# A fused decoder layer on one core: one engine order changed, one input split a period ahead, loops written out

## The chip, the cores and the metric

The kernel runs on one core of one Trainium2 chip. The metric is the device time of one execution in microseconds (us). Engines are named as the profile names them: PE is TensorE, PEld its weight loads, DVE is VectorE, ACT is ScalarE, POOL is GpSimd, SP the engine that issues the transfers. Each engine has its own instruction stream, in order, and they meet through semaphores alone.

## What is computed

Three stages on x of 8 batches x 256 tokens x 512 features, each followed by a residual and a layer norm:

```
i, f, g = x Wi^T, x Wf^T, x Wg^T
h       = scan(h' = sigmoid(f) h + silu(i) (1 - sigmoid(f)))
xg      = h silu(g);  y = xg rsqrt(mean(xg^2) + eps) w_norm;  x1 = LN(x + y Wo)
x2      = LN(x1 + wkv(w, u, k = x1, v = ctx))          # a second scan over the tokens
x3      = LN(x2 + quantised MLP(x2))                   # 512 -> 2 x 1408 -> silu(gate) up -> 512
```

The MLP rounds its input, its hidden row and its weights to 127 steps per row; the kernel multiplies the rounded whole numbers in bf16 and scales behind the product. The first stage's projections are made in three products each, high x high, low x high and high x low, from inputs that are split into a rounded high part and the rest.

## The kernel before

Tiles are 128 tokens; a batch has TB = 2 of them, so 16 tiles n in all. The work is pipelined by hand over three batches. Iteration b runs the MLP of batch b, the middle stage of batch b + 1 and the first stage of batch b + 2, and every engine has a function `iteration` that lists its own steps in order. Ahead of the loop there is a long written-out part (weights are loaded, split or quantised, turned and kept; batches 0 to 2 are started), then `iteration(1, 1)`, then a hardware loop (`Fori(2, 6, 2)`) whose body holds iterations b and b + 1, since the buffers alternate. Batches 6 and 7 end in a written-out tail. In the loop, semaphores are awaited against values worked out from the loop's register.

The steps that the change and the prediction touch:

- PE (line 655, `iteration`): `mlp_up` in three chunks of columns for each of the two tiles, gate and up halves (line 579, 16 products of 128x128 by 512 columns in a full chunk); `turn_keys` (L534); six projections `project` (L476); `turn_hidden` (L599); `mlp_down` (L612) of a tile, 11 products in two parts of 6 and 5 (`PARTS`), each behind its own copy of turned hidden values; `turn_values` (L545); `project_out` (L476) for the tiles 0 and 1; `sum_squares` (L510, 16 tiny products with ones); `turn_inputs` (L554, 8 transposes in 16 bit), which waits for `round_2`.
- ACT (line 984): `split_x` (L835, high part of the next input, 128x1024), `silu` (L929), table loads (L978, L982), `exponential`, `read_projection` (L821 and L824), `split_states` (L841), `square` (L862), `round_hidden` (L936), `read_hidden` (L943), `normalise_3` (L907), `round_2` (L913), `read_inputs` (L920, turned inputs to xqT), `normalise_1` (L901).
- POOL (line 1288): `split_x` (L1189, low part: forget - x_high), `hidden` (L1257, gate x up), `rstd_2` (L1244, L1247), `rms_scale` (L1206), `rstd_1` (L1212 to L1221), `residual_3`, `past_values`, `newton`.
- DVE (line 1693): `scale_products` (L1585, L1588), `weigh_inputs`, `recurrence` (L1440, the scan in the tile `forget`, which also receives the transposed input), `gating` (L1446), `split_states` (L1451), `residual_2`, `layer_norm_2`, `normalise_2` (L1555, two halves of 128x512), `mean_square` (L1457), `scale_2`, `residual_1` (L1465), `layer_norm_1`, `read_down` (L1637), `hidden_max_row` (L1604), `hidden_scale` (L1619 to L1626).
- SP (line 406): transfers of the transposed input (`load_xT`, into `forget`), the context (`load_c`), the input (`load_x`) and two stores of 128 tokens. Each waits for its buffer, and those behind it wait too.

The order at the end of PE's iteration and the start of the next is the one the prediction speaks of:

```
                project_out(b + 2, 0)
                sum_squares(b + 2)
                project_out(b + 2, 1)
                mlp_down(n, 0)
                turn_inputs(b + 1)      # then mlp_up(b + 1, ..., 0, [0])
```

Of the kernel before, what the change touches and what calls it, by code (L numbers as in the profile page):

```python
# [26 lines left out]
BATCHES, T, D, I = 8, 256, 512, 1408  # L27
# [16 lines left out]
PARTS = [(0, (IB + 1) // 2), ((IB + 1) // 2, IB // 2)]  # L44
# [11 lines left out]
def decoder_layer(nc, xT, x, cT, wfT, wiT, wgT, w_norm, woT, w, u, w_gate_up, w_down, out,  # L56
                  scratch):
    ctx = ExitStack()
    with ctx:
# [286 lines left out]
        def _(sp):  # L346
            def load_xT(b):
                wait(sp, h_ready, b)
                sp.dma_start(forget[:, :, :], xT[b]).then_inc(xT_loaded, 16)
# [56 lines left out]
            def iteration(b):  # L406
                load_xT(b + 2)
                load_c(b + 1)
                store(b * TB - 2, b - 1, 0)
                load_x(b + 2)  # L410
                store(b * TB - 1, b - 1, 1)
# [38 lines left out]

            with sp.Fori(1, BATCHES - 2) as b:
                iteration(b)
# [15 lines left out]
        def _(pe):  # L468
# [135 lines left out]

            def mlp_down(n, t):

                s = (t + NC) % 2
                pe.wait_ge(mlp_read, chunks_read(n))
                for part, (first, count) in enumerate(PARTS):
# [4 lines left out]
                last.then_inc(down_done, 1)  # L614

# [39 lines left out]
            def iteration(b, par):  # L655
# [20 lines left out]
                turn_hidden(n, 0, 0)  # L676
                turn_hidden(n, 0, 1)
                project_out(b + 2, 0)
                sum_squares(b + 2)
                project_out(b + 2, 1)  # L680
                mlp_down(n, 0)
                turn_inputs(b + 1)

            pe.wait_ge(identity_ready, 1)
# [81 lines left out]

            iteration(1, 1)
            with pe.Fori(2, BATCHES - 2, 2) as b:
                iteration(b, 0)
                iteration(b + 1, 1)  # L770

# [36 lines left out]
        def _(act):  # L808
# [175 lines left out]
            def iteration(b, par):  # L984
                n = b * TB
                split_x(b + 2)
                silu(b, par, 0, [0])
# [31 lines left out]
                read_hidden(n, 0, 1)  # L1019
                silu(b, par, 1, [2])  # L1020
                normalise_3(n - 1, 1)
                round_2(b + 1, 1 - par, 0)
# [91 lines left out]
            silu(0, 0, 0, [2])  # L1114
            square(2)
            round_hidden(0, 0, 0)
            round_hidden(0, 0, 1)
# [9 lines left out]

            iteration(1, 1)
            with act.Fori(2, BATCHES - 2, 2) as b:
                iteration(b, 0)  # L1130
                iteration(b + 1, 1)

# [53 lines left out]
        def _(pool):  # L1186
# [101 lines left out]
            def iteration(b, par):  # L1288
                n = b * TB
                split_x(b + 2)  # L1290
                residual_3(n - 2, 1 - par, 0)
# [14 lines left out]
                rms_scale(b + 2)  # L1306
                hidden(b, 1, [2])
                rstd_1(b + 2)

# [50 lines left out]
            hidden(0, 0, [2])  # L1360
            rstd_2(1)
            rms_scale(2)
            hidden(0, 1, [0])
# [3 lines left out]

            iteration(1, 1)
            with pool.Fori(2, BATCHES - 2, 2) as b:
                iteration(b, 0)  # L1370
                iteration(b + 1, 1)

# [32 lines left out]
        def _(dve):  # L1405
# [422 lines left out]

            iteration(1, 1)
            with dve.Fori(2, BATCHES - 2, 2) as b:  # L1830
                iteration(b, 0)
                iteration(b + 1, 1)

# [111 lines left out]
```

## Time and profile before

| | |
|---|---|
| median of 3 executions | 435.67 us (434.51 to 436.34) |
| the profiled execution | 435.61 us |
| its span, first to last instruction | 433.8 us |
| mean granted TensorE clock | 0.977 of 2.4 GHz |
| PE busy | 386.3 us, 89% |
| DVE busy | 364.1 us, 84% |
| ACT busy | 320.3 us, 74% |
| POOL busy | 217.1 us, 50% |
| transfers | 31.75 MB, 73 GB/s on average |

The 1.8 us between span and time lie around the first and last instruction. Busy shares are means over a start in which weights come in, a repeating middle (from about 148 to 368 us, batches 1 to 5) and a tail with little PE work. In a timeline row the first two numbers are start and length of a merged run of like instructions, `x4` their count, and the bracket the idle time of the engine ahead of it and what ended it. Lengths of merged matmuls carry a pipeline's tail of about 0.17 us.

### The profile page before, as it was taken

The page shows a single profiled execution, that of the slowest core. Times are in us where ns is not written, and L with a number is a line of the kernel's source. Part 1 is how long each engine was busy: PE and PEld are TensorE (multiplying, and loading weights), DVE is VectorE, ACT ScalarE, POOL GpSimd, SP SyncE. Part 2 cuts the span into 40 slices and gives each one's busy share as a digit, 9 for nine tenths or more (in the row PEclk, how much of TensorE's full clock was granted, in tenths as well). Part 3 has the DMA queues.
Part 4 walks back from the last instruction along what each step waited for, and adds up shares of the span by engine and source line. Part 5 has one row for each costly group of instructions (what it writes and reads, how often), then busy time and mean ns, then how long its engine had stood idle before and what let it go on. Part 6 is the DMA issues. An engine that isn't in the chain of part 4 may idle for free.

```text
span 433.8 us, 8164 instructions
## 1 busy us (share of the span) xinstructions
PE 386.3 (89%) x2906; PEld 305.5 (70%) x2906; DVE 364.1 (84%) x620; ACT 320.3 (74%) x422; POOL 217.1 (50%) x266
## 2 busy tenths in 40 slices
PE   7898989989898899989998999899989998577873
PEld 7797889877876597759774977597758776333431
DVE  3879698493998799989898998899888989899684
ACT  3668678639926799589957996699759884986671
POOL 1554465243542865457435942594258436626451
PEclk9899999989999999999999999999999999888998
DMA  7946350663020002030203020302030202000101
GB/s 261 351 165 244 115 214 20 232 50 91 2 98 1 2 0 75 2 122 2 73 2 122 3 74 0 121 0 73 0 121 0 73 0 73 2 25 2 48 13 62
DMA packets 12843, 31.75 MB, mean 73 GB/s; under 512 B 2038, under 2 KB 5132, under 8 KB 12812
## 3 DMA queue, kind: packets, MB, share of 16 engines
q1 hardware_dynamic: 12812, 31.35, 21.8%
q8 instruction: 18, 0.29, 0.3%
q14 instruction: 13, 0.11, 0.1%
HBM read 27.14 MB, written 4.21 MB: 72 GB/s over the span
## 4 chain that ended last, share of the span: by engine, by line
PE 43%; ACT 18%; DVE 15%; issue 12%; POOL 5%; DMA 3%; SPq 1%; ACTq 0%; POOLq 0%; DVEq 0%
PE proj_ps L476 24%; PE slot_ps L579 10%; PE slot_ps L612 3%; PE turn_ps L510 2%; POOL ring L1257 2%; ACT xqT L920 2%; DVE ring L1585 2%; ACT L978 2%; ACT hqT L943 2%; DMA ring<-w_gate_up_dram 2%; DMA ring<-w_down_dram 2%; DVE ring L1588 2%; ACT turn_ps L883 2%; ACT L982 1%; DVE xg_low L1451 1%
## 5 line engine op out<-in xcount | busy, mean ns | idle before, releaser
L579 PE MATMUL slot_ps<-w1q,xqT 128*128 128x512 bf16 (+1 forms) x384 | 83.1, 367 | 10.5 <-ACT xqT L920 7.6
L1257 POOL TENSOR_TENSOR ring<-ring 128x512 f32<-128x512 f32 (+1 forms) x48 | 60.5, 1263 | 33.6 <-ACT ring L929 33.6
L579 PEld LDWEIGHTS slot_ps<-w1q,xqT 128*128 128x128 bf16 x384 | 36.8, 99 | 48.8 <-issue 7.9
L476 PE MATMUL proj_ps<-x_high,proj_high 128*128 128x256 f32 x384 | 65.8, 294 | 2.1 <-DVE inp L1465 2.0
L476 PE MATMUL proj_ps<-x_high,proj_low 128*128 128x256 f32 x384 | 62.5, 285 | 0.0
L476 PE MATMUL proj_ps<-x_low,proj_high 128*128 128x256 f32 x384 | 62.4, 284 | 0.0
L476 PEld LDWEIGHTS proj_ps<-x_high,proj_high 128*128 128x128 f32 x384 | 54.2, 192 | 3.9 <-issue 2.4
L476 PEld LDWEIGHTS proj_ps<-x_high,proj_low 128*128 128x128 f32 x384 | 53.9, 193 | 0.0
L476 PEld LDWEIGHTS proj_ps<-x_low,proj_high 128*128 128x128 f32 x384 | 53.4, 191 | 0.0
L929 ACT ACTIVATE ring<-ring,zero_bias,x_scale 128x512 f32<-128x512 f32 (+1 forms) x48 | 36.9, 774 | 12.3 <-DVE ring L1585 11.8
L612 PE MATMUL slot_ps<-w2q,hqT 128*128 128x512 bf16 x176 | 42.1, 388 | 4.3 <-ACT hqT L943 3.3
L1585 DVE TENSOR_TENSOR ring<-slot_ps,scale_rows 128x512 f32<-128x512 f32 (+1 forms) x48 | 30.7, 639 | 17.0 <-PE slot_ps L579 17.0
L1232 POOL TENSOR_TENSOR den<-den,q_state 128x512 f32<-128x512 f32 x16 | 26.4, 1657 | 34.7 <-ACT q_state L889 34.4
L1199 POOL TENSOR_SCALAR ring<-ring,row_inv 128x512 f32<-128x512 f32 (+1 forms) x26 | 27.2, 1060 | 19.1 <-DVE row_inv L1680 19.1
L936 ACT ACTIVATE ring<-ring,round_bias,hid_inv 128x768 f32<-128x768 f32 (+1 forms) x32 | 29.6, 965 | 7.1 <-DVE hid_inv L1626 7.1
L612 PEld LDWEIGHTS slot_ps<-w2q,hqT 128*128 128x128 bf16 x176 | 16.2, 99 | 25.1 <-issue 5.2
L1588 DVE TENSOR_TENSOR ring<-slot_ps,scale_rows 128x512 f32<-128x512 f32 (+1 forms) x48 | 30.5, 636 | 0.0
L1189 POOL TENSOR_TENSOR x_low<-forget,x_high 128x1024 fp32r<-128x1024 f32 x7 | 16.6, 2370 | 26.7 <-ACT x_high L835 26.7
L1604 DVE TENSOR_REDUCE hid_top<-ring 128x1 f32<-128x1408 f32 x15 | 24.2, 1611 | 5.5 <-POOL ring L1257 5.4
L943 ACT ACTIVATE hqT<-slot_ps,half_bias 128x768 bf16<-128x768 f16 (+1 forms) x32 | 25.3, 836 | 4.1 <-PE slot_ps L599 4.1
L1227 POOL TENSOR_TENSOR num<-num,c_sb 128x512 f32<-128x512 f32 x16 | 20.3, 1284 | 11.7 <-ACT num L873 11.4
L1674 DVE TENSOR_REDUCE row_max<-ring 128x2 f32<-128x1024 f32 (+1 forms) x15 | 19.8, 1317 | 5.9 <-DMA ring<-w_down_dram 4.8
(133 smaller groups left out, 845.7 us busy)
## 6 DMA issues: line engine op xcount, KB each, us to landing
ring<-w_gate_up_dram SPq DMA_DIRECT2D x11, 512.0 KB, 5.0
forget<-xT_dram SPq DMA_DIRECT2D x8, 512.0 KB, 3.9
x_sb<-x_dram SPq DMA_DIRECT2D x8, 512.0 KB, 3.7
c_sb<-cT_dram SPq DMA_DIRECT2D x8, 512.0 KB, 4.1
out_dram<-z SPq DMA_DIRECT2D x16, 256.0 KB, 2.0
ring<-w_down_dram SPq DMA_DIRECT2D x4, 704.0 KB, 5.7
scale_rows<-scratch_dram SPq DMA_DIRECT2D x2, 704.0 KB, 5.9
x<-wfT_dram SPq DMA_DIRECT2D x2, 512.0 KB, 5.6
```

The lines of the kernel that those rows point to most:

```text
L476: last = nc.tensor.matmul(out, a, b, start=(i == 0), stop=(i == len(terms) - 1))
L579: last = nc.tensor.matmul(slot_ps[:, s, half * 512:half * 512 + width], xqT[:, par, d, t * P:(t + 1) * P], w1q[:, d, half * I + at:half * ...
L612: last = nc.tensor.matmul(slot_ps[:, s, 0:D], hqT[:, i, :], w2q[:, i, :], start=(i == 0), stop=(i == IB - 1))
L929: nc.scalar.activation(g, g, ACT.Silu, bias=zero_bias[:, :], scale=x2_scale[:, par, t:t + 1]).then_inc(silu_ready, 1)
L936: nc.scalar.activation(h, h, ACT.Identity, bias=round_bias[:, :], scale=hid_inv[:, t:t + 1]).then_inc(hid_rounded, 1)
L943: nc.scalar.activation(hqT[:, first:first + count, :].rearrange("p i t -> p (i t)"), part_16((t + 1 + NC) % 2, part), ACT.Identity, bias=h ...
L1199: last = nc.gpsimd.tensor_scalar(rows[:, a, :], rows[:, a, :], row_inv[:, c:c + 1], ROUND, ALU.mult, ALU.add)
L1232: nc.gpsimd.tensor_tensor(blocks(den, h), blocks(den, h), blocks(rec_copy, h), ALU.mult).then_inc(newton_ready, 1)
L1257: nc.gpsimd.tensor_tensor(hid, hid, gate_buf[:, at:at + width], ALU.mult).then_inc(hid_ready, 1)
L1585: nc.vector.tensor_tensor(gate_buf[:, at:at + width], slot_ps[:, s, 0:width], scale_rows[:, at:at + width], ALU.mult).then_inc(gate_scaled, 1)
L1588: nc.vector.tensor_tensor(hid_buf(t)[:, at:at + width], slot_ps[:, s, 512:512 + width], scale_rows[:, I + at:I + at + width], ALU.mult).th ...
L1604: nc.vector.tensor_reduce(hid_top[:, :], hid_buf(t)[:, 0:I], AX.X, ALU.max, apply_absolute_value=True).then_inc(hid_top_ready, 1)
```

## The change

PE does `sum_squares(b + 2)` ahead of both `project_out`, and `turn_inputs(b + 1)` between the two parts of `mlp_down(n, 0)`; `mlp_down` takes the parts as an argument for that. `split_x` for batch b + 3 moves from the start of iteration b + 1 to the end of iteration b on ACT (ahead of `normalise_3`) and POOL (ahead of `rstd_1`), and that of batch 3 into the part ahead of the loop (ACT behind `square(2)`, POOL behind `rstd_2(1)`). Its transfer is issued in iteration b, behind the first store, and `load_x` ahead of that store. The hardware loops of all five engines become Python loops, so each iteration's instructions are written out, with constants.

```
@@ -404,10 +404,11 @@
                 sp.dma_start(out[b, par], y3[:, par, :]).then_inc(out_stored[par], 16)
 
             def iteration(b):
-                load_xT(b + 2)
                 load_c(b + 1)
+                load_x(b + 2)
                 store(b * TB - 2, b - 1, 0)
-                load_x(b + 2)
+                if b + 3 < BATCHES:
+                    load_xT(b + 3)
                 store(b * TB - 1, b - 1, 1)
 
 
@@ -448,7 +449,8 @@
             spread_scales(2)
             load_x(2)
 
-            with sp.Fori(1, BATCHES - 2) as b:
+            load_xT(3)
+            for b in range(1, BATCHES - 2):
                 iteration(b)
 
 
@@ -602,16 +604,19 @@
                                                identity16[:, :])
                 last.then_inc(hq_turned, 1)
 
-            def mlp_down(n, t):
+            def mlp_down(n, t, parts=(0, 1)):
 
                 s = (t + NC) % 2
-                pe.wait_ge(mlp_read, chunks_read(n))
-                for part, (first, count) in enumerate(PARTS):
+                if parts[0] == 0:
+                    pe.wait_ge(mlp_read, chunks_read(n))
+                for part in parts:
+                    first, count = PARTS[part]
                     pe.wait_ge(hq_ready, 2 * n + part + 1)
                     for i in range(first, first + count):
                         last = nc.tensor.matmul(slot_ps[:, s, 0:D], hqT[:, i, :], w2q[:, i, :],
                                                 start=(i == 0), stop=(i == IB - 1))
-                last.then_inc(down_done, 1)
+                if parts[-1] == 1:
+                    last.then_inc(down_done, 1)
 
             def turn_rows(q):
 
@@ -675,11 +680,12 @@
                 turn_values(b + 1, 1)
                 turn_hidden(n, 0, 0)
                 turn_hidden(n, 0, 1)
+                sum_squares(b + 2)
                 project_out(b + 2, 0)
-                sum_squares(b + 2)
                 project_out(b + 2, 1)
-                mlp_down(n, 0)
+                mlp_down(n, 0, (0,))
                 turn_inputs(b + 1)
+                mlp_down(n, 0, (1,))
 
             pe.wait_ge(identity_ready, 1)
 
@@ -764,10 +770,8 @@
             turn_inputs(1)
             mlp_down(0, 0)
 
-            iteration(1, 1)
-            with pe.Fori(2, BATCHES - 2, 2) as b:
-                iteration(b, 0)
-                iteration(b + 1, 1)
+            for b in range(1, BATCHES - 2):
+                iteration(b, b % 2)
 
 
             mlp_up(6, 0, 0, [0])
@@ -983,7 +987,6 @@
 
             def iteration(b, par):
                 n = b * TB
-                split_x(b + 2)
                 silu(b, par, 0, [0])
                 exp_tables()
                 exponential(b + 1, 0)
@@ -1018,6 +1021,8 @@
                 read_hidden(n, 0, 0)
                 read_hidden(n, 0, 1)
                 silu(b, par, 1, [2])
+                if b + 3 < BATCHES:
+                    split_x(b + 3)
                 normalise_3(n - 1, 1)
                 round_2(b + 1, 1 - par, 0)
                 round_2(b + 1, 1 - par, 1)
@@ -1113,6 +1118,7 @@
             split_states(2)
             silu(0, 0, 0, [2])
             square(2)
+            split_x(3)
             round_hidden(0, 0, 0)
             round_hidden(0, 0, 1)
             silu(0, 0, 1, [0])
@@ -1125,10 +1131,8 @@
             silu(0, 0, 1, [2])
             normalise_1(2)
 
-            iteration(1, 1)
-            with act.Fori(2, BATCHES - 2, 2) as b:
-                iteration(b, 0)
-                iteration(b + 1, 1)
+            for b in range(1, BATCHES - 2):
+                iteration(b, b % 2)
 
 
             exp_tables()
@@ -1287,7 +1291,6 @@
 
             def iteration(b, par):
                 n = b * TB
-                split_x(b + 2)
                 residual_3(n - 2, 1 - par, 0)
                 hidden(b, 0, [0])
                 past_values(b + 1, 0)
@@ -1305,6 +1308,8 @@
                 rstd_3(n - 1, 1)
                 rms_scale(b + 2)
                 hidden(b, 1, [2])
+                if b + 3 < BATCHES:
+                    split_x(b + 3)
                 rstd_1(b + 2)
 
             nc.gpsimd.memset(ones[:, :], 1.0)
@@ -1359,16 +1364,15 @@
             hidden(0, 0, [1])
             hidden(0, 0, [2])
             rstd_2(1)
+            split_x(3)
             rms_scale(2)
             hidden(0, 1, [0])
             hidden(0, 1, [1])
             rstd_1(2)
             hidden(0, 1, [2])
 
-            iteration(1, 1)
-            with pool.Fori(2, BATCHES - 2, 2) as b:
-                iteration(b, 0)
-                iteration(b + 1, 1)
+            for b in range(1, BATCHES - 2):
+                iteration(b, b % 2)
 
 
             residual_3(10, 1, 0)
@@ -1826,10 +1830,8 @@
             layer_norm_1(2)
             read_down(0, 0, 0)
 
-            iteration(1, 1)
-            with dve.Fori(2, BATCHES - 2, 2) as b:
-                iteration(b, 0)
-                iteration(b + 1, 1)
+            for b in range(1, BATCHES - 2):
+                iteration(b, b % 2)
 
 
             hidden_max_row(5, 1)
```

## Rows read from the trace of the kernel before

**Rows 1.** Windows, PE alone: stretch, length, PE busy (instructions), granted clock, DMA share, GB/s.
```profile
148.00:176.00 28.00, 27.95 (x217) 1.00 0.09 30
283.00:311.00 28.00, 27.82 (x216) 1.00 0.08 28
```

**Rows 2.** Timeline of PE, loop: start us, us, engine line, instruction, xcount [idle before].
```profile
278.29 3.62 PE L579 MATMUL slot_ps<-w1q,xqT 128*128 128x512 bf16 x16 [1.30 <-ACT xqT L920]
...
311.46 1.20 PE L476 MATMUL proj_ps<-wo_high,xg_high 128*128 128x512 f32 x4 [0.64 <-DVE xg_low L1451]
...
318.98 2.55 PE L612 MATMUL slot_ps<-w2q,hqT 128*128 128x512 bf16 x11
...
323.25 1.03 PE L579 MATMUL slot_ps<-w1q,xqT 128*128 128x512 bf16 x4 [1.28 <-ACT xqT L920]
```

**Rows 3.** Timeline of ACT over the same period.
```profile
278.32 1.52 ACT L901 ACTIVATE x<-inp,shift,rstd 128x512 f32<-128x512 f32 x2 [0.18 <-POOL shift L1221]
...
281.05 0.81 ACT L929 ACTIVATE ring<-ring,zero_bias,x_scale 128x512 f32<-128x512 f32 x1 [0.17 <-DVE ring L1585]
...
292.83 0.69 ACT L824 ACTIVATE inp<-proj_ps,zero_bias 128x512 f32<-128x512 f32 x1 [1.04 <-PE proj_ps L476]
...
317.92 0.82 ACT L907 ACTIVATE z<-z,shift,rstd 128x512 f32<-128x512 f32 x1 [2.63 <-POOL shift L1278]
318.86 1.52 ACT L913 ACTIVATE num<-x,round_bias,x_inv 128x512 f32<-128x512 f32 x2
322.01 1.11 ACT L920 ACTIVATE xqT<-turn_ps,half_bias 128x1024 bf16<-128x1024 f16 x1 [1.63 <-PE turn_ps L554]
```

**Rows 4.** Timeline of DVE over the same period.
```profile
307.54 1.25 DVE L1446 TENSOR_TENSOR inp<-inp,gate 128x1024 f32<-128x1024 f32 x1 [0.67 <-ACT gate L824]
...
315.19 1.95 DVE L1555 TENSOR_SCALAR x<-num,mv,rstd 128x512 f32<-128x512 f32 x2 [0.18 <-POOL rstd L1247]
```

**Rows 5.** Timeline of ACT behind the loop: round_2 and read_inputs of batch 7.
```profile
398.03 1.51 ACT L913 ACTIVATE num<-x,round_bias,x_inv 128x512 f32<-128x512 f32 x2
400.25 1.11 ACT L920 ACTIVATE xqT<-turn_ps,half_bias 128x1024 bf16<-128x1024 f16 x1 [0.71 <-PE turn_ps L554]
```

**Rows 6.** Timeline of POOL in the loop.
```profile
280.96 2.37 POOL L1189 TENSOR_TENSOR x_low<-forget,x_high 128x1024 fp32r<-128x1024 f32 x1 [2.67 <-ACT x_high L835]
...
315.12 1.27 POOL L1257 TENSOR_TENSOR ring<-ring 128x512 f32<-128x512 f32 x1
...
321.97 0.20 POOL L1212 TENSOR_TENSOR ve<-mv,eps_col 128x2 f32<-128x2 f32 x1 [2.40 <-DVE mv L1477]
```

**Rows 7.** Timeline of DVE behind the loop: read_down and the last of hidden_scale.
```profile
366.76 0.74 DVE L1637 SCALAR_TENSOR_TENSOR z<-slot_ps,hid_scale,scale_rows 128x512 f32<-128x512 f32 x1
...
369.51 0.21 DVE L1626 TENSOR_SCALAR hid_inv<-hid_rec,x_scale 128x1 f32<-128x1 f32 x1
```

**Rows 8.** DMA issues of the page: KB each, median us from issue to landing.
```profile
forget<-xT_dram SPq DMA_DIRECT2D x8, 512.0 KB, 3.9
```

**Rows 9.** Timelines of ACT, POOL, DVE and PE ahead of the loop.
```profile
131.99 1.84 ACT L936 ACTIVATE ring<-ring,round_bias,hid_inv 128x768 f32<-128x768 f32 x2 [4.29 <-DVE hid_inv L1626]
...
131.76 0.69 POOL L1247 TENSOR_TENSOR rstd<-ve,minus_half 128x2 f32<-128x2 f32 x1
...
138.18 0.69 POOL L1206 TENSOR_TENSOR rms<-msq,minus_half 128x2 f32<-128x2 f32 x1 [5.72 <-DVE msq L1457]
...
132.49 1.00 DVE L1555 TENSOR_SCALAR x<-num,mv,rstd 128x512 f32<-128x512 f32 x2 [0.53 <-POOL rstd L1247]
...
134.75 1.47 PE L579 MATMUL slot_ps<-w1q,xqT 128*128 128x384 bf16 x8 [0.79 <-DVE ring L1588]
```

**Rows 10.** Timeline of PE behind the loop.
```profile
377.93 0.82 PE L599 MATMUL slot_ps<-identity,ring 128*128 128x128 f16 x6 [3.95 <-ACT ring L936]
...
380.92 3.72 PE L612 MATMUL slot_ps<-w2q,hqT 128*128 128x512 bf16 x11 [0.16 <-ACT hqT L943]
```

**Rows 11.** Source query of L1465: durations ns min/median/max, first and last start, forms.
```profile
L1465 DVE SCALAR_TENSOR_TENSOR inp<-proj_ps,rms,x_sb x16: 732/750/752, 44.4 to 364.6; 128x512 f32<-128x512 f32 x16
```

More of the change, by code:

```diff
@@ L406, in iteration @@
             def iteration(b):
-                load_xT(b + 2)
                 load_c(b + 1)
+                load_x(b + 2)
                 store(b * TB - 2, b - 1, 0)
-                load_x(b + 2)
+                if b + 3 < BATCHES:
+                    load_xT(b + 3)
                 store(b * TB - 1, b - 1, 1)
@@ L449, in _ @@
             load_x(2)
-            with sp.Fori(1, BATCHES - 2) as b:
+            load_xT(3)
+            for b in range(1, BATCHES - 2):
                 iteration(b)
@@ L603, in turn_hidden, with mlp_down @@
                 last.then_inc(hq_turned, 1)
-            def mlp_down(n, t):
+            def mlp_down(n, t, parts=(0, 1)):
                 s = (t + NC) % 2
-                pe.wait_ge(mlp_read, chunks_read(n))
-                for part, (first, count) in enumerate(PARTS):
+                if parts[0] == 0:
+                    pe.wait_ge(mlp_read, chunks_read(n))
+                for part in parts:
+                    first, count = PARTS[part]
                     pe.wait_ge(hq_ready, 2 * n + part + 1)
@@ L613, in mlp_down @@
                                                 start=(i == 0), stop=(i == IB - 1))
-                last.then_inc(down_done, 1)
+                if parts[-1] == 1:
+                    last.then_inc(down_done, 1)
             def turn_rows(q):
@@ L677, in iteration @@
                 turn_hidden(n, 0, 1)
+                sum_squares(b + 2)
                 project_out(b + 2, 0)
-                sum_squares(b + 2)
                 project_out(b + 2, 1)
-                mlp_down(n, 0)
+                mlp_down(n, 0, (0,))
                 turn_inputs(b + 1)
+                mlp_down(n, 0, (1,))
             pe.wait_ge(identity_ready, 1)
@@ L765, in _ @@
             mlp_down(0, 0)
[L767 to L770, printed above, removed]
+            for b in range(1, BATCHES - 2):
+                iteration(b, b % 2)
             mlp_up(6, 0, 0, [0])
@@ L985, in iteration @@
                 n = b * TB
-                split_x(b + 2)
                 silu(b, par, 0, [0])
@@ L1020, in iteration @@
                 silu(b, par, 1, [2])
+                if b + 3 < BATCHES:
+                    split_x(b + 3)
                 normalise_3(n - 1, 1)
@@ L1115, in _ @@
             square(2)
+            split_x(3)
             round_hidden(0, 0, 0)
@@ L1126, in _ @@
             normalise_1(2)
[L1128 to L1131, printed above, removed]
+            for b in range(1, BATCHES - 2):
+                iteration(b, b % 2)
             exp_tables()
@@ L1289, in iteration @@
                 n = b * TB
-                split_x(b + 2)
                 residual_3(n - 2, 1 - par, 0)
@@ L1307, in iteration @@
                 hidden(b, 1, [2])
+                if b + 3 < BATCHES:
+                    split_x(b + 3)
                 rstd_1(b + 2)
@@ L1361, in _ @@
             rstd_2(1)
+            split_x(3)
             rms_scale(2)
@@ L1366, in _ @@
             hidden(0, 1, [2])
[L1368 to L1371, printed above, removed]
+            for b in range(1, BATCHES - 2):
+                iteration(b, b % 2)
             residual_3(10, 1, 0)
@@ L1827, in _ @@
             read_down(0, 0, 0)
[L1829 to L1832, printed above, removed]
+            for b in range(1, BATCHES - 2):
+                iteration(b, b % 2)
             hidden_max_row(5, 1)
```

## The prediction

> **What bounds the kernel now.** I read the PE rows of the windows first, then the timelines of the four engines over one batch period of the loop, then the same engines just ahead of the loop and behind it. In the repeating part TensorE is nearly always at work: 27.82 of 28 us in a looped stretch and 27.95 of 28 in the same stretch of batch 1, which is straight-line code [rows 1]. One period, from the first gate/up product to the next one, takes 323.25 - 278.29 = 44.96 us, and there are two holes in it: 0.64 us before `project_out`, waiting for VectorE's xg_low, and 1.28 us before the first `mlp_up`, where PE has turned the inputs and waits for ScalarE to copy them out [rows 2]. So a period is PE's work plus a wait that PE's own order causes: `mlp_down` stands ahead of `turn_inputs`, and nothing stands behind it.
>
> Call R the end of `round_2`, which releases `turn_inputs`: 318.86 + 1.52 = 320.38 [rows 3]. From the period's first product (278.29) to R there are 42.09 us, in this chain: 14.54 to ScalarE's read of the third projection (292.83, where it had been idle for 1.04, so PE is the later one), then ScalarE, VectorE and ScalarE back to back with holes of 0.7 at most [rows 2 to 4]. From R to the next first product the old order takes 44.96 - 42.09 = 2.87 us.
>
> **The change, part by part.**
>
> *`turn_inputs` between the two parts of `mlp_down`.* The six products of part 0 take 6 x 0.217 = 1.30 us (eleven take 2.55 less about 0.17 of tail, [rows 2]). They end at 318.98 + 1.30 = 320.28, before R, so the turn now starts at R. Behind the loop there is a turn that is not queued behind other work: `round_2` ends at 398.03 + 1.51 = 399.54 and ScalarE's copy starts at 400.25, 0.71 later [rows 5]. The copy takes 1.11, and from its end to PE's product there are 323.25 - (322.01 + 1.11) = 0.13 in the loop [rows 2, 3]. R to first product becomes 0.71 + 1.11 + 0.13 = 1.95; the five products of part 1 (1.09) lie under the copy. The period becomes 42.09 + 1.95 = 44.04, a gain of 0.92 us.
>
> Who is late next? `read_down` on VectorE now waits for part 1: 0.71 for the turn with its handovers and 1.09 of products, so R + 1.8. VectorE's statistics are done at R + 1.6 (POOL's rstd starts on them at 321.97, [rows 6]), so it waits 0.2 us. From `read_down` to the free gate product takes 369.72 - 366.76 = 2.96 [rows 7], and the gate product that releases silu is another 0.7: silu at R + 5.5. ScalarE's front of silu, exponentials and two projection reads takes 292.83 - 1.04 - 281.05 = 10.74 [rows 3], ready at R + 16.2. PE delivers the third projection at R + 1.95 + 14.54 = R + 16.5. PE is still the later, by 0.3: the gain holds, but no more than 0.3 above it is to be had.
>
> *`sum_squares` ahead of `project_out`.* It waits for ScalarE's squares instead of xg_low, both made from the same product at about the same time, and can win at most the first hole of 0.64 [rows 2]. But the 7.52 us of products up to 318.98 and part 0 would then only end before 320.28 and wait longer for R; mean_square is queued behind normalise_2 on VectorE and is not late. Should the squares come later than xg_low, there are 0.10 us before part 0 passes R. Worth nothing now; bounds -0.1 and +0.1 a period.
>
> *`split_x` one period ahead.* ScalarE's 1.13 us leave the start of the period and land ahead of `normalise_3`, where it is idle for 2.63 [rows 3]. POOL's 2.37 us leave 280.96 and land before rstd_1, where POOL is idle for 2.40 [rows 6]; that fits within 0.1 us. The normalised rows behind it are there at 278.32 + 1.52 = 279.84, and `turn_keys` wants them 3.62 us behind the first product, at 281.91 [rows 2, 3]: of these 2.07 us some 1.0 are left when PE starts 0.92 earlier. Nothing is gained at the start of the period, since silu waits for VectorE; it only keeps x_low from becoming late for a PE that starts 0.9 earlier. Its DMA needs the recurrence's end, before 307.54, and a store ahead of it whose rows are ready sooner, and takes 3.9 to land [rows 4, 8], against a split at about 315. SP's load of x now follows that of c at once; both buffers are free by then, and c is read only behind silu and the table load. Zero for both.
>
> *Loops written out.* Constant waits can save the 0.08 by which the loop's handover is longer than 0.05, at one place of the chain; more code has to be fetched, but batch 1 already runs as straight code with PE as full as in the loop [rows 1]. I take 0; bounds: -0.3 in all, and above it the 0.13 by which the two stretches differ in each of four periods, +0.5.
>
> *The new `split_x(3)` ahead of the loop.* On ScalarE it falls into 4.29 us of idling. On POOL it stands right behind rstd_2(1), which ends at 132.45, ahead of a 5.72 us wait: free for POOL. But the same rstd_2 releases VectorE's normalise_2, at 132.49 [rows 9]. In the loop the same pair meets: a POOL product of 1.27 us starts at 315.12, 0.07 ahead of normalise_2, and the two VectorE halves take 1.95 us [rows 4, 6]. Ahead of the loop, with POOL quiet, they take 1.00 [rows 9]. The first half would be done at 315.74 and is done 0.95 later, 0.30 after the POOL product's end at 316.39. Behind a POOL instruction of 2.37 us that starts at about 132.43, the first half ends at 132.43 + 2.37 + 0.30 = 135.10 instead of 133.04: +2.06 us. Everything here hangs on it: PE waits for the scaled product behind normalise_2 (0.79 at 134.75, [rows 9]), then come sum_squares, residual, hidden maximum, and silu of batch 1. No slack is in it. Bounds: 0 if VectorE starts first; 2.4 if it waits out the whole instruction and then runs in full.
>
> The Trainium skill ("SBUF — State Buffer", section "SBUF: two separate sides") gives GpSimd and a VectorE operation in a two-port mode one shared port pair, which whoever starts first keeps for its whole instruction. By that rule the price is 2.0 us with POOL first and nothing with VectorE first, the sum 434.0 or 432.0. By that rule, the trace agrees as far as POOL first goes; no row here shows VectorE first against an instruction of this length.
>
> **Sum.** R of batch 1 is set by the ScalarE-VectorE chain, not by PE: it gains nothing and moves by +2.06. From there to R of batch 5 there are four periods: -4 x 0.92 = -3.7. The fifth early start (batch 6) gives nothing: its second product group stands behind `turn_keys`, whose rows come 279.84 - 278.29 = 1.55 us after the old first product, so 2.5 after the new one, with one product group of 1.8 us ahead of it. Bounds for it: 0 to 0.9. Total -1.6. The profiled execution took 435.61 us, 0.06 under the median of 435.67: forecast **434.0 us**.
>
> **Rivals.**
> *No collision ahead of the loop* (VectorE starts first, or waits less): 435.67 - 3.7 = 432.0. For: the two are released by one event, 0.06 apart. Against: POOL was first in the loop, where it too had no other wait.
> *TensorE's clock falls ahead of the loop.* PE's idle before 134.75 grows from 0.79 to 2.83. Behind the loop, after 3.95 us of idling, eleven products took 3.72 instead of 2.55 us [rows 2, 10]: half the clock, 1.2 of 2.4 GHz. If the 3 us around sum_squares run at half clock, 1.3 to 1.7 us come on top: 435.5. Against: this idle is shorter, and batch 1 runs at full clock behind it now [rows 1].
> *Slower: x_low blocks VectorE in the loop too.* Its new place is over residual_1 and the statistics. If residual_1 waited it out as normalise_2 does, about 2 us, `read_down` would come at R + 3.6, silu at R + 7.3, the third read at R + 18.0 instead of 16.5: period 45.5, +0.6 x 4 = 2.4, and 2.06 before it: 440.1. It decides as soon as VectorE loses over 0.5 us (0.2 of idling and 0.3 of PE's lead). Against: residual_1 took 0.732 to 0.752 in all sixteen cases, with and without POOL beside it [rows 11].
> *The loop gains nothing* (VectorE or POOL's Newton step, which has 0.67 us of slack before the gating product [rows 4], takes over): 435.67 + 2.0 = 437.7.
>
> **Numbers.** Forecast 0.50, no collision 0.20, clock 0.15, slower by x_low 0.05, no gain in the loop 0.10. A measurement tells about 0.5% from no change, 2.2 us: 433.5 and 437.85 are the limits. The forecast's own range is 433.0 to 434.9, so a quarter of it counts as faster, with all of the no-collision case: 0.32. Slower are x_low's case and a third of the last, 0.08. Same: 0.60. The range runs from 431.6 (no collision, with the 0.3 of the written-out loops) to 436.9 (clock, or half the loop's gain missing).
>
> **What would show it.** Right: periods of about 44.0 us, the hole before `mlp_up` between 0.1 and 0.3 us with one of some 0.1 to 0.5 before `turn_inputs`; the two halves of normalise_2(1) at about 3.0 us with x_low started just ahead; `round_2` of batch 1 about 2 us later than before, of batch 5 about 1.7 earlier. Wrong: normalise_2(1) at 1.0 us; periods above 44.3; residual_1 above 0.9 us; a granted clock under 1 between 136 and 145.

## The result, and the profile after

The changed kernel takes 450.46 us (median of 4 executions, 447.81 to 452.41); the kernel before took 435.28 beside it (434.51 to 436.34, 4 executions). The ratio is 1.033, 95% interval 1.030 to 1.037. It is slower by 15 us where 434.0 had been forecast, with 0.08 given to slower at all.

| | before | after |
|---|---|---|
| profiled execution, its span | 435.61, 433.8 us | 451.22, 449.2 us |
| mean granted clock of TensorE | 0.977 | 0.948 |
| first product of batch 1 (gate/up) | 141.71 | 145.34 |
| period of batches 1 to 5 | 46.64, 44.96, 44.98, 44.96, 44.89 | 49.17, 44.87, 46.39, 47.99, 48.02 |
| behind the fifth period | 65.7 | 67.4 |

So of 15.4 us of span, 3.6 come ahead of the loop, 10.0 in its five periods (236.44 against 226.43), 1.8 behind. The 3.6 and the 1.8 are less firm than the 10.0: in nine profiled kernels that have no collision ahead of the loop, the kernel before among them, the first product of batch 1 lies anywhere from 139.13 to 141.71, and *loops_only*, with the old order, already takes 66.8 behind the fifth period. I did not follow up the part behind. The periods are not alike, which a wait alone would make them. The timeline of PE over the end of one period, in the changed kernel:

```profile
316.51 1.04 PE L547 MATMUL turn_ps<-identity,num 128*128 128x128 f32 x8
317.59 0.78 PE L601 MATMUL slot_ps<-identity,ring 128*128 128x128 f16 x11
320.04 2.73 PE L512 MATMUL turn_ps<-ones,gate 128*128 128x1 f32 x16 [1.67 <-DVE num L1540]
322.62 2.05 PE L478 MATMUL proj_ps<-wo_high,xg_high 128*128 128x512 f32 x4
324.47 1.91 PE L478 MATMUL proj_ps<-wo_high,xg_low 128*128 128x512 f32 x4
326.18 1.82 PE L478 MATMUL proj_ps<-wo_low,xg_high 128*128 128x512 f32 x4
327.83 1.09 PE L478 MATMUL proj_ps<-wo_high,xg_high 128*128 128x512 f32 x4
```

Two things are to be seen. First, `sum_squares` (L512) waits 1.67 us, and not for the squares but for `num` of L1540, VectorE's `residual_2`. Second, behind that hole the same work takes longer: four products of `project_out` 1.8 to 2.05 us instead of 1.1 to 1.2. That is the lower clock, as the windows say (stretch, length, PE busy, granted clock, DMA share, GB/s), first over the slow products, then over a whole period without a fall, one with a short one and one with a long one:

```profile
319.50:327.50 8.00, 7.46 (x28) 0.59 0.06 21
194.51:239.38 44.87, 42.82 (x298) 1.00 0.13 45
239.38:285.77 46.39, 44.35 (x297) 0.96 0.14 47
285.77:333.76 47.99, 45.95 (x297) 0.93 0.14 46
```

VectorE over the same stretch shows why the releaser is late, and who waits next:

```profile
317.47 1.23 DVE L1455 TENSOR_TENSOR xg_low<-inp,xg_high 128x1024 fp32r<-128x1024 f32 x1
318.61 1.28 DVE L1540 TENSOR_TENSOR num<-x,turn_ps 128x512 f32<-128x512 f32 x2
...
328.04 0.75 DVE L1469 SCALAR_TENSOR_TENSOR inp<-proj_ps,rms,x_sb 128x512 f32<-128x512 f32 x1 [1.75 <-PE proj_ps L478]
330.84 0.75 DVE L1469 SCALAR_TENSOR_TENSOR inp<-proj_ps,rms,x_sb 128x512 f32<-128x512 f32 x1 [2.06 <-PE proj_ps L478]
```

`residual_2` stands behind `split_states` (L1455) in VectorE's order and ends at 319.89; PE was ready at 318.37, ScalarE's squares (L866) at 317.34 + 1.14 = 318.48. `sum_squares` may not start before `residual_2`, because its sums go into the bank of turn_ps that `residual_2` reads the turned values from: `wait(pe, z2_ready, 2 * b)` of batch b + 2 is `residual_2` of batch b + 1. In the old order the 3 us of `project_out(b + 2, 0)` lay on top of it, and it was never seen.

ScalarE's `read_inputs`, which had waited 1.63 [rows 3], now waits 4.76, since PE comes late to the turn. Timeline of ACT:

```profile
326.31 1.52 ACT L917 ACTIVATE num<-x,round_bias,x_inv 128x512 f32<-128x512 f32 x2
332.60 1.11 ACT L924 ACTIVATE xqT<-turn_ps,half_bias 128x1024 bf16<-128x1024 f16 x1 [4.76 <-PE turn_ps L556]
```

Ahead of the loop the forecast collision is there, in POOL and DVE, and behind it the lower clock, in PE (granted clock 0.50 from 137.23 to 141.63):

```profile
131.25 2.38 POOL L1193 TENSOR_TENSOR x_low<-forget,x_high 128x1024 fp32r<-128x1024 f32 x1
...
131.33 3.04 DVE L1559 TENSOR_SCALAR x<-num,mv,rstd 128x512 f32<-128x512 f32 x2 [0.54 <-POOL rstd L1251]
...
135.63 1.81 PE L581 MATMUL slot_ps<-w1q,xqT 128*128 128x384 bf16 x8 [2.83 <-DVE ring L1592]
137.23 3.41 PE L512 MATMUL turn_ps<-ones,gate 128*128 128x1 f32 x16
140.51 1.33 PE L601 MATMUL slot_ps<-identity,ring 128*128 128x128 f16 x11
```

`normalise_2(1)` takes 3.04 instead of 1.00 [rows 9], and the idle time before PE's product 2.83 instead of 0.79. The sixteen products of `sum_squares` take 3.41 instead of 1.84, as they do in the kernel before:

```profile
136.06 1.84 PE L510 MATMUL turn_ps<-ones,gate 128*128 128x1 f32 x16
```

### The profile page after: what moved, and what is told of

It is laid out like the page before. It is cut to its first block, busy times and chain, and to the rows that moved or that the text cites. A ratio compares the mean times of both kernels' runs of the same rounds, so it can differ in the third digit from the quotient of the medians.

```text
span 449.2 us, 7782 instructions
## 1 busy us (share of the span) xinstructions
PE 396.8 (88%) x2884; PEld 314.9 (70%) x2906; DVE 367.0 (82%) x620; ACT 320.5 (71%) x422; POOL 219.2 (49%) x266
## 4 chain that ended last, share of the span: by engine, by line
PE 36%; ACT 21%; DVE 17%; issue 14%; POOL 6%; DMA 3%; SPq 1%; POOLq 0%; DVEq 0%; ACTq 0%
PE proj_ps L478 22%; PE slot_ps L581 6%; PE turn_ps L512 3%; POOL ring L1261 3%; ACT hqT L947 2%; ACT L982 2%; DVE ring L1589 2%; ACT L986 2%; ACT ring L933 2%; DMA ring<-w_gate_up_dram 2%; DVE inp L1450 2%; DVE num L1540 2%; DVE ring L1592 2%; ACT q_state L893 2%; DMA ring<-w_down_dram 2%
## 5 line engine op out<-in xcount | busy, mean ns | idle before, releaser
L581 PE MATMUL slot_ps<-w1q,xqT 128*128 128x512 bf16 (+1 forms) x377 | 80.2, 362 | 6.5 <-DVE ring L1592 3.8
L1236 POOL TENSOR_TENSOR den<-den,q_state 128x512 f32<-128x512 f32 x16 | 28.0, 1767 | 31.1 <-ACT q_state L893 31.1
L512 PE MATMUL turn_ps<-ones,gate 128*128 128x1 f32 x128 | 19.9, 285 | 8.3 <-DVE num L1540 8.3
L512 PEld LDWEIGHTS turn_ps<-ones,gate 128*128 128x128 f32 x128 | 20.0, 243 | 9.4 <-issue 9.2
```

Source lines behind the costliest of these rows:

```text
L512: last = nc.tensor.matmul(sumsq_ps[:, t:t + 1], sq[:, c, t * P:(t + 1) * P], ones[:, 0:1], start=(c == 0), stop=(c == DB - 1))
L581: last = nc.tensor.matmul(slot_ps[:, s, half * 512:half * 512 + width], xqT[:, par, d, t * P:(t + 1) * P], w1q[:, d, half * I + at:half * ...
L1236: nc.gpsimd.tensor_tensor(blocks(den, h), blocks(den, h), blocks(rec_copy, h), ALU.mult).then_inc(newton_ready, 1)
```

## The experiments

Twelve kernels, in four groups; each group had its own runs of the kernel before beside it. Ratios are to the kernel before, with 95% intervals. "First period" is the one from the first product of batch 1; it is longer or shorter by what stands ahead of it, so I compare the four behind it. A fall is a stretch of the lower clock; an undisturbed period has none.

**First group: which part of the change costs, and which gains.** The kernel before took 434.8 here.

*sumsq_back*: the changed kernel, one line moved.

```
+                project_out(b + 2, 0)
                 sum_squares(b + 2)
-                project_out(b + 2, 0)
```

> The changed kernel with sum_squares put back behind the first project_out; all else stays (turn_inputs between the parts, split_x a period ahead, loops written out). Theory W, that the loss comes from sum_squares waiting for residual_2 in its new place, with TensorE's clock falling in that hole: the loss of each period goes and the forecast's periods of 44.0 us appear; what is left is the 2.0 us of normalise_2 ahead of the loop and up to 2 us of half clock there, so 434 to 436.5 us. Rival F, that written-out loops cost (code has to come in): 445 or more. Rival S, that split_x's new places cost: 445 or more too.

435.16 us (10 executions), ratio 0.999 [0.995, 1.002]. The periods are 43.92, 43.91, 43.91, 43.91. PE in one of them:

```profile
267.64 1.16 PE L478 MATMUL proj_ps<-wo_high,xg_high 128*128 128x512 f32 x4 [0.42 <-issue]
...
270.51 1.84 PE L512 MATMUL turn_ps<-ones,gate 128*128 128x1 f32 x16
...
275.34 1.24 PE L616 MATMUL slot_ps<-w2q,hqT 128*128 128x512 bf16 x5
276.72 0.62 PE L556 MATMUL turn_ps<-identity,num 128*128 128x128 f16 x8
277.18 1.24 PE L616 MATMUL slot_ps<-w2q,hqT 128*128 128x512 bf16 x5
278.55 1.68 PE L581 MATMUL slot_ps<-w1q,xqT 128*128 128x512 bf16 x7
```

All of the loss goes with one line. The turn is hidden as worked out: a hole of 0.14 before it (276.72 less 276.58) and 0.13 before `mlp_up`. Ahead of the loop its profiled execution still has the collision and, behind it, the lower clock: `sum_squares` 3.41, `mlp_down` 3.64 for ten products.

*sumsq_only*: the kernel before with that one line moved, hardware loops and all.

```
-                project_out(b + 2, 0)
                 sum_squares(b + 2)
+                project_out(b + 2, 0)
```

> The kernel before, with hardware loops and all, and only sum_squares moved ahead of both project_out. Theory W: the hole ahead of it grows from 0.64 to about 1.7 us in each of five periods, and where the clock falls to half behind it another 1.7 us or more: 441 to 450 us. Rivals F and S: within 0.5 us of the kernel before, 435.3.

449.11 us (4), ratio 1.032 [1.025, 1.038], periods 47.57, 46.06, 47.58, 47.48. This one move makes the whole loss by itself:

```profile
271.11 0.79 PE L599 MATMUL slot_ps<-identity,ring 128*128 128x128 f16 x11
273.64 1.92 PE L510 MATMUL turn_ps<-ones,gate 128*128 128x1 f32 x16 [1.74 <-DVE num L1536]
```

*filled*: the changed kernel, and PE turns a constant 22 times in the wait.

```
+                pe.wait_ge(xg_low_ready, b + 3)
+                pe.wait_ge(proj_read, b * PROJ + 2 * PROJ + 5)
+                keep_busy(22, proj_ps[:, 0, 0:P // 2])
                 sum_squares(b + 2)
```

> The changed kernel with 22 small transposes into a free PSUM bank ahead of sum_squares, once xg_low is there, so that PE is busy while it waits for residual_2. The wait stays, only the idling goes. Theory W with the clock as the larger part: the granted clock stays at full in the loop, sum_squares takes 1.8 us instead of 2.7 to 3.3, periods 45.0 to 45.4, total 439 to 442 us. If the clock is not part of it: no change from 450.

440.37 us (4), ratio 1.014 [1.005, 1.022], periods 44.86, 44.87, 44.85, 46.41. `sum_squares` still waits for `residual_2`, and three of four periods have the length of the one undisturbed period of the changed kernel, 44.87. So the wait costs 44.87 - 43.91 = 0.96 us a period, and what lies above is the clock.

*loops_only*: the kernel before, with `for b in range(1, BATCHES - 2)` for the hardware loops of all engines.

> The kernel before with the hardware loops of all engines written out and nothing else changed. Theory W: 435.3 less 0 to 0.4 us. Rival F: 440 or more.

433.81 us (10), ratio 0.996 [0.993, 1.000], periods 44.68, 44.68, 44.68, 44.70 against 44.96. Written-out loops are worth 0.28 us a period, and no cost of the longer code shows in the periods. Of the 0.28, 0.2 is the hole before `project_out`: 0.42 instead of 0.64 [rows 2], in all five periods; in the kernel before, batch 1, which is straight code there too, has 0.42 already. Constants in the waits and the loop's own work went together, so this run does not say which of the two gives the gain.

**Second group: can the wait be shortened, and what is the rest worth?** The kernel before took 435.67.

*swap*: the changed kernel with VectorE's `residual_2(b + 1, 0)` and `(b + 1, 1)` moved ahead of `split_states(b + 2)`.

> The changed kernel, sum_squares ahead as in it, but VectorE does both residual_2 ahead of split_states instead of behind. Theory W (the wait for residual_2 is the cause): sum_squares starts 1.2 us earlier, project_out behind it finds xg_low ready, the clock stays at full in the loop, and the period is 43.9 to 44.2 us, so 434 to 437 us in all, like the kernel with sum_squares back (435.2). If it were the place of sum_squares itself and not that wait: 445 or more.

*swap_apart*: `swap`, and the collision ahead of the loop taken away: POOL waits until `normalise_2(1)` is done.

```
             rstd_2(1)
+            pool.wait_ge(x2_ready, 4)
             split_x(3)
```

> Both: residual_2 ahead of split_states, and split_x(3) on POOL behind normalise_2(1), with the change's order on PE. Theory W and the collision: 431 to 432.5 us, the fastest of all, 0.8% under the kernel before.

*back_apart*: `sumsq_back` with the same wait on POOL.

> sum_squares back behind the first project_out, and ahead of the loop POOL's split_x(3) waits until normalise_2(1) is done, so the two don't meet. If the collision costs what I forecast (2.06 us) and brings the clock down ahead of the loop: normalise_2(1) takes 1.0 us instead of 3.0, full clock there, 431 to 432.5 us. If the collision costs nothing: 435.2 as with sum_squares back alone.

*turn_only*: the kernel before with written-out loops and `turn_inputs` between the parts of `mlp_down`; `split_x` and the transfers stay where they were.

> The kernel before with loops written out and turn_inputs between the parts of mlp_down, nothing else: split_x stays at the start of the period, so there is no collision ahead of the loop. x_low is then late for a PE that starts 0.9 us earlier: by my reckoning at R + 8.2 against R + 7.8, a new wait of about 0.4 us before the first project; period 44.2 to 44.5, total 432 to 433.5 us against 433.8 with the loops written out alone. If the early turn gives nothing: 433.8.

| | us (executions) | ratio | periods 2 to 5 |
|---|---|---|---|
| swap | 440.75 (4) | 1.012 [1.008, 1.016] | 43.95, 46.96, 45.39, 46.97 |
| swap_apart | 435.87 (10) | 1.002 [0.998, 1.006] | 43.95, 43.95, 46.95, 45.38 |
| back_apart | 430.68 (4) | 0.988 [0.985, 0.992] | 43.92, 43.91, 43.93, 43.92 |
| turn_only | 432.66 (6) | 0.992 [0.989, 0.995] | 44.38, 44.39, 44.38, 44.72 |

`back_apart` is the fastest, faster than both kernels. `swap` and `swap_apart` missed: moving `residual_2` takes the hole down to 0.66 and the undisturbed period to 43.95, as expected, but the clock still falls. The same stretch in two periods of `swap_apart`, the first at the full clock (1.00 from 264 to 270), the second not (0.50 from 309 to 315), with the same hole ahead:

```profile
261.58 0.77 PE L601 MATMUL slot_ps<-identity,ring 128*128 128x128 f16 x11
263.02 1.92 PE L512 MATMUL turn_ps<-ones,gate 128*128 128x1 f32 x16 [0.66 <-DVE num L1541]
264.80 1.18 PE L478 MATMUL proj_ps<-wo_high,xg_high 128*128 128x512 f32 x4
...
306.97 2.30 PE L512 MATMUL turn_ps<-ones,gate 128*128 128x1 f32 x16 [0.66 <-DVE num L1541]
309.13 2.05 PE L478 MATMUL proj_ps<-wo_high,xg_high 128*128 128x512 f32 x4
```

`turn_only` says what the turn is worth without the early `split_x`, 44.68 - 44.38 = 0.30 us a period, and what `split_x` one period ahead (with its transfer) adds: 44.38 - 43.92 = 0.46. Left where it was, the split comes late for the earlier PE; the timeline of POOL:

```profile
276.08 0.20 POOL L1221 TENSOR_TENSOR shift<-neg_mean,rstd 128x2 f32<-128x2 f32 x1
278.94 2.37 POOL L1189 TENSOR_TENSOR x_low<-forget,x_high 128x1024 fp32r<-128x1024 f32 x1 [2.67 <-ACT x_high L837]
```

x_low is there at 281.31, and PE's first product that needs the split input starts at 281.41, 6.01 behind the period's first product (275.40); in *sumsq_back* it is 5.50 (284.05 - 278.55). The profile names no releaser for PE's idle time there (0.21, "issue"), so that it is x_low is read from these times.

**Third group: the hole or the work around it, and the part ahead of the loop.** The kernel before took 435.16.

*swap_filled*: `swap_apart`, with ten turns of a constant in the hole of 0.66.

```
+                pe.wait_ge(proj_read, b * PROJ + 2 * PROJ + 5)
+                keep_busy(10, proj_ps[:, 0, 0:P // 2])
                 sum_squares(b + 2)
```

> swap_apart with ten small transposes of a constant into the free bank of the eviction tile just ahead of sum_squares, so that TensorE works in the hole of 0.7 us that is left there. If it is the idle hole that takes the clock away, no period of the loop falls to the lower level and the time is 431 to 432.5 us (swap_apart 435.9, whose undisturbed periods were 43.95). If it is the light work itself (transposes and one-column products one behind the other), the falls stay and the time stays at 435 to 437 us.

434.09 us (10), ratio 0.996 [0.994, 0.999], periods 45.38, 43.96, 43.94, 45.38. Expected was all or nothing, and it came in between; but its trace answers the question. Here PE has no listed idle time from the turned values on (4.16 us busy of 4.30, at a granted clock of 1.00), and the clock falls all the same, to 0.55 over the 3.6 us behind 221.40:

```profile
217.10 1.04 PE L547 MATMUL turn_ps<-identity,num 128*128 128x128 f32 x8
218.18 0.77 PE L601 MATMUL slot_ps<-identity,ring 128*128 128x128 f16 x11
218.79 0.72 PE L658 MATMUL proj_ps<-identity 128*128 128x128 f16 x10
219.60 1.92 PE L512 MATMUL turn_ps<-ones,gate 128*128 128x1 f32 x16
221.38 1.76 PE L478 MATMUL proj_ps<-wo_high,xg_high 128*128 128x512 f32 x4
222.94 1.91 PE L478 MATMUL proj_ps<-wo_high,xg_low 128*128 128x512 f32 x4
```

*back_warm*: `sumsq_back`, and 44 turns of a constant in PE's wait behind the collision ahead of the loop.

```
+            pe.wait_ge(z2_ready, 4)
+            keep_busy(44, turn_ps[:, 0:P // 2])
             mlp_up(0, 0, 1, [2])
```

> sumsq_back with small transposes of a constant in TensorE's wait ahead of the loop, which keep it working while VectorE's normalise_2(1) and GpSimd's split_x(3) still collide. It splits the 4.5 us between sumsq_back (435.2) and back_apart (430.7) into the collision itself and the clock behind it. If the collision costs about 2 us by itself and the rest is the clock, 432 to 433.5 us with the products ahead of the loop at the upper level. If the clock is all of it, 430.5 to 431.5; if it is none, 435.

433.75 us (10), ratio 0.996 [0.994, 0.999], just above the expected 432 to 433.5. `normalise_2(1)` takes 3.05 as in `sumsq_back`, and `sum_squares` is back at 1.84, but `mlp_down` still takes 4.22. The interval overlaps that of `sumsq_back`, so the share of the clock in the 4.5 us between `sumsq_back` and `back_apart` is not measured well; that collision and clock together make them is (0.999 against 0.988, intervals apart). Nor does the 1.84 show that the turns kept the clock up: in the traces of `filled` and `swap`, which have the collision and the same idle time of PE behind it and nothing in it, `sum_squares` takes 1.84 as well:

```profile
135.35 1.47 PE L581 MATMUL slot_ps<-w1q,xqT 128*128 128x384 bf16 x8 [2.84 <-DVE ring L1592]
136.66 1.84 PE L512 MATMUL turn_ps<-ones,gate 128*128 128x1 f32 x16
```

These rows are of `swap`. Its first product of batch 2 comes at 188.11, against 185.83 in `swap_apart`: without a fall the collision costs 2.3 us. In `sumsq_back`, with the fall, it comes 4.85 later than in `back_apart` (190.72 against 185.87).

*after_apart*: the changed kernel with POOL's wait, and nothing else.

> The changed kernel with GpSimd's split_x(3) held behind VectorE's normalise_2(1), so that the two do not collide ahead of the loop. My theory: the same 2 to 4.5 us go as between sumsq_back and back_apart, 446 to 448.5 us, and the loop keeps its falls to the lower clock, since the wait ahead of sum_squares stays. The rival, that the lower clock ahead of the loop is what brings the falls in the loop about, expects periods of 44.9 without a fall and a time of 436 to 439 us.

449.65 us (6), ratio 1.025 [1.020, 1.030], against 1.033 [1.030, 1.037] of the changed kernel. The time missed the expected 446 to 448.5. By the ratios it is 0.8% or some 3.6 us less than the changed kernel, but the intervals touch and the medians are only 0.8 apart (its executions scatter from 445.69 to 452.88), so this gain is not shown; between `sumsq_back` and `back_apart` it is. `normalise_2(1)` is at 1.01, the first product of batch 1 at 141.71 as in the kernel before, and the periods are 46.42, 47.99, 48.00, 48.01. These answer the question: the rival, that the lower clock ahead of the loop brings about that in the loop, is out.

**Fourth: full-width work in the same hole.** The kernel before took 435.0.

*swap_heavy*: `swap_filled` with three products of 512 columns for the ten turns.

```
-                keep_busy(10, proj_ps[:, 0, 0:P // 2])
+                for _ in range(3):
+                    nc.tensor.matmul(proj_ps[:, 0, :], w1q[:, 0, 0:P], w1q[:, 0, 0:512],
+                                     start=True, stop=True)
```

> swap_filled with three products of 512 columns in place of the ten small transposes, so that the hole of 0.7 us ahead of sum_squares is filled for the same time, but with full-width work. swap_filled kept the clock in two of five periods only, although nothing was left of the hole. If it is the unbroken light work (transposes, then one-column products) that takes the clock away, no period or one falls now, every period is about 43.95 and the time is 431 to 432.5 us. If the position of sum_squares matters for another reason, two or three of the five periods fall as in swap_filled (45.4) and the time is 434 to 436 us.

432.03 us (10), ratio 0.992 [0.989, 0.995], periods 43.95, 43.95, 45.39, 43.92. One fall is left, in the profiled execution, which at 434.59 is the slowest of the ten.

```profile
218.50 0.77 PE L601 MATMUL slot_ps<-identity,ring 128*128 128x128 f16 x11
219.11 0.81 PE L685 MATMUL proj_ps<-w1q 128*128 128x512 bf16 x3
219.94 1.92 PE L512 MATMUL turn_ps<-ones,gate 128*128 128x1 f32 x16
221.72 1.18 PE L478 MATMUL proj_ps<-wo_high,xg_high 128*128 128x512 f32 x4
```

A profile has only five such stretches: with the first period counted, the falls are 2 of 5 in `swap_apart`, 3 in `swap_filled`, 1 in `swap_heavy` and 1 in `filled`, which gives no order. So I put the mean granted clock over all executions beside it. It takes in the whole kernel, and `after` alone of the five has the collision ahead of the loop; without it, `after_apart` has 0.950 and 449.65:

| what stands between the turns and `sum_squares` | kernel | mean clock | us |
|---|---|---|---|
| hole of 1.67 | after | 0.953 | 450.46 |
| hole of 0.66 | swap_apart | 0.967 | 435.87 |
| ten turns | swap_filled | 0.974 | 434.09 |
| three full products | swap_heavy | 0.980 | 432.03 |
| hole of 0.42, `project_out(b + 2, 0)` | back_apart | 0.982 | 430.68 |

`swap_apart` and `swap_heavy` are apart by their intervals (1.002 against 0.992); the two steps between them are not, each for itself.

## Why the prediction was wrong, point by point

**The step that failed** is "It waits for ScalarE's squares instead of xg_low, both made from the same product at about the same time, and can win at most the first hole of 0.64", with its end: "Worth nothing now; bounds -0.1 and +0.1 a period." The function has two waits in the loop, and I priced one. The other, on `z2_ready`, was covered by 3 us of products in the old order, so no view of the trace before shows it as a wait. Its price could have been read there, on VectorE in the kernel before:

```profile
311.14 1.28 DVE L1536 TENSOR_TENSOR num<-x,turn_ps 128x512 f32<-128x512 f32 x2
```

`residual_2` ended at 312.42 (311.14 + 1.28), while PE was ready for the next step 0.64 before 311.46, at 310.82 [rows 2]. That is a hole of 1.6 us, against 1.67 measured. The wait alone costs 0.96 a period (*filled* against *sumsq_back*), the clock behind it 0, 1.5 or 3.1 more.

**The sum that replaces it**, from `back_apart`, which has no wait, no collision and no fall: from its first product of batch 1 to the end of the fifth period it takes 221.45 us, against 226.43 before. To get to 236.44 after, 15.0 are missing: 5 x 0.96 = 4.8 for the wait, and 10.2 for the clock. Beside `sumsq_back`, which has the collision too, it comes out alike: the fifth period ends at 366.37 there and at 381.78 in the changed kernel, 15.4 later, 4.8 for the wait and 10.6 for the clock. So two thirds of the loss are the clock that fell around the wait, and the sum had no term for it. I had a rival for the lower clock ahead of the loop and none for it in the loop, where the trace of before had shown it at 1.00 [rows 1]. That trace held a warning that I did not use. Ahead of the loop one short idle time went with a fall, and another did not:

```profile
89.50 0.94 PE L476 MATMUL proj_ps<-x_high,proj_high 128*128 128x256 f32 x4 [1.97 <-DVE inp L1465]
...
147.89 1.47 PE L579 MATMUL slot_ps<-w1q,xqT 128*128 128x384 bf16 x8 [1.69 <-DVE ring L1588]
```

The granted clock was 0.50 from 90 to 92 us, behind the first, and 1.00 from 147 to 155, around the second. Nor does the first always bring a fall: in `loops_only` the same step, with the same 1.97 ahead, takes 0.72 instead of 0.94.

**The turn between the parts of `mlp_down`** was right in mechanism and close in size. Periods of 44.04 were forecast, 43.92 measured; but they are made up otherwise. From `loops_only` to `sumsq_back` it is 44.68 - 43.91 = 0.77, not 0.92, and of that 0.30 come with the turn alone and 0.46 only with the early `split_x` (*turn_only*). Both holes were forecast, some 0.1 to 0.5 before the turn (0.14) and 0.1 to 0.3 before `mlp_up` (0.13).

**Loops written out** were undersized: 0.28 us a period, where I had allowed 0.3 for all periods together because I looked at one place of the chain only; 0.2 of it lie at another, the hole before `project_out`. In the periods the longer code costs nothing that shows, as forecast.

**`split_x` one period ahead** held: nothing was won at the start of the period by itself, and without it x_low is late for the earlier PE, by 0.46 a period (*turn_only*). The rival in which x_low blocks VectorE in the loop did not come: `residual_1` (L1469) takes 0.732 to 0.752 in all sixteen cases, as before [rows 11], and the one at 328.04 above has x_low (2.40 us from 326.94) running beside it.

**The collision ahead of the loop** was right in place and size: 3.0 forecast, 3.04 measured, with x_low started 0.08 ahead. The Trainium skill ("SBUF — State Buffer", section "SBUF: two separate sides") has the loser of the shared port pair wait for the winner's whole instruction. By the letter of that, `normalise_2` would begin its work at POOL's end, 133.63, and be 133.63 - 131.33 = 2.30 us late (an estimate); the prediction put this rule at 2.0, which is the price from the rows and not the rule's. The trace agrees with the blocking but for 0.26 us: 2.04 come on top, and the first half ends at 133.92 (its 2.586 us are the longest of L1559), 0.29 behind POOL's end, where a half alone takes about 0.55. From [rows 4, 6] the prediction had worked out 0.30. A wait on POOL for `x2_ready` takes the collision away (`normalise_2(1)` 1.00 in `back_apart`) and costs nothing that shows, since POOL is idle behind it.

**The clock ahead of the loop** was a rival at 0.15, priced 1.3 to 1.7 us. It came: `sum_squares` alone takes 3.41 - 1.84 = 1.57 more, and the turns behind it 0.56 and 0.45 on top, so it was also priced too low. It does not always come: of the four profiled executions with the collision and nothing in PE's wait, `after` and `sumsq_back` have it, `filled` and `swap` do not. I argued that an idle time of 2.83 us is shorter than the 3.95 behind the loop [rows 10]; that was no argument, since the trace of before has no row in which 2.83 us of idling leave the clock alone, and one in which 1.97 went with a fall.

With the failed step taken out, the kernel is `sumsq_back`, and 434.0 was forecast for it: it takes 435.16, ratio 0.999 [0.995, 1.002]. The rival without collision, forecast at 432.0, is `back_apart`: 430.68. That `sumsq_back` comes so near 434.0 is partly luck: it holds at least some 2.6 us of lower clock ahead of the loop (the 1.57, 0.56 and 0.45) that the sum left out, and 4 x 0.28 = 1.1 us of gain from the written-out loops that it left out too.

## What to carry to other kernels

When a step is moved up in an engine's order, list every semaphore that it waits for, and find for each where the releasing step stands in its own engine's order at the new time: a wait that never shows in the trace of before may only have been covered by the work that the step now passes. Here a step of many tiny products right behind a run of transposes went with falls of the clock, and a full `project_out` between them with none (`back_apart`); try that order, and price a new hole in such a stretch at the lower clock too. Before a transfer of work to GpSimd, look for a VectorE instruction like `normalise_2` (fp32 tensor_scalar in SBUF) that the same event releases, and let one wait for the other.

## What the runs showed of the hardware

The clock fell to its lower level (1.2 of 2.4 GHz) with no listed idle time of TensorE ahead: in `swap_filled` it worked through eight turns of values, eleven of hidden values, ten of a constant and sixteen one-column products, and the full-width products behind them took 1.76 and 1.91 instead of 1.18 and 1.10 us. The same sequence left the clock alone in other periods of the same execution (266.76 1.18, 267.78 1.10 for such groups). A fall costs about 1.45 or 3.0 us of a period here. The Trainium skill ("TensorE: Matmul & The Clock Gate", section "A second HAM failure mode: psum-queue depth-cycling") describes a clock that alternates where TensorE idles briefly and often between groups of products. The runs agree in that falls come with a single short hole a period (0.66 us in `swap_apart`), and go further, since in `swap_filled` they come with none. A hole by itself is not enough either: those of 1.28 to 1.30 us before every `mlp_up` [rows 2] and the 1.69 at 147.89, with products of 256 to 512 columns behind, left the clock at 1.00, and so did the 1.67 in one period of the changed kernel. What stays open is which of the light steps counts for how much, what decides between a period that falls and its equal that does not, and why `filled`, with twice the turns, had one fall in four periods where `swap_filled` had two: neither the number of profiles nor the runs tell these apart.

Loops written out, with constants in the waits instead of values of a loop's register, gave 0.28 us a period (44.96 to 44.68), and the hole before `project_out` went from 0.64 to 0.42, where the profile no longer names a releaser ("issue").
